# Probability transposes, value and relative matmuls of an attention loop placed one unit later in a hand-written order, and the output store one step later

## What is computed

```python
Q, K, V = (proj(Wq), proj(Wk), proj(Wv))             # 16 x 16 heads x 1024 x 16
scores = jnp.einsum('bhqd,bhkd->bhqk', Q, K) / SCALE
idx = clip(k - q, -256, 256) + 256
scores = scores + jnp.einsum('bhqd,qkd->bhqk', Q, pek[idx]) / SCALE
scores = jnp.where(causal[None, None], scores, -jnp.inf)
attn = jax.nn.softmax(scores, axis=-1)
out = jnp.einsum('bhqk,bhkd->bhqd', attn, V)
out = out + jnp.einsum('bhqk,qkd->bhqd', attn, pev[idx])
...
x = _layernorm(x + out @ Wo.T)
x = _layernorm(x + ffn(x))
```

## Time and profile before

| | |
|---|---|
| median of 3 runs | 5945.27 us (5935.37 to 5958.6) |
| the profiled execution | 5937.08 us; its span 5935.4 us |
| outside the span | 1.7 us |
| attention stage | from about 0.48 ms to 4.72 ms |
| busy over the span | PE 87%, DVE 64%, ACT 58%, POOL 31% |
| mean granted PE clock | 0.972 |

### The profile page before, as it was taken

How to read it: one execution, slowest core, us unless ns; L and a number is a source line. 1 busy time by engine, 2 the same in 40 slices (tenths; PEclk the granted TensorE clock), 3 DMA queues, 4 the chain that set the end, 5 groups by cost and what they waited for, 6 DMA issues and landing times. The chain is left out here.

```text
span 5935.4 us, 143051 instructions
## 1 busy us (share of the span) xinstructions
PE 5156.7 (87%) x49460; PEld 3407.6 (57%) x49460; DVE 3809.4 (64%) x8777; ACT 3447.7 (58%) x7512; POOL 1838.5 (31%) x2516
## 2 busy tenths in 40 slices
PE   9977888888888888888888888888888799999999
PEld 5545555555555555555555555555555556666655
DVE  5546676676667766676667666776677645555554
ACT  4436777777777777777777777777677511111111
POOL 4443333333333333333333333333333211111111
PEclk9989999999999999999999999999999999999999
DMA  7888999999999999899999999899999711111111
GB/s 225 253 225 278 287 299 292 285 294 297 287 290 294 302 292 298 286 292 295 294 290 294 290 293 291 289 296 296 283 293 291 248 54 57 57 57 57 57 57 39
DMA packets 653784, 1417.28 MB, mean 239 GB/s; under 512 B 64004, under 2 KB 362088, under 8 KB 640872
## 3 DMA queue, kind: packets, MB, share of 16 engines
q1 hardware_dynamic: 653160, 1409.10, 75.7%
HBM read 737.46 MB, written 671.35 MB: 237 GB/s over the span
## 5 line engine op out<-in xcount | busy, mean ns | idle before, releaser
L791 ACT ACTIVATE a_prob<-a_neg_s,a_neg_max 128x384 f32<-128x384 f32 (+1 forms) x1792 | 1076.1, 601 | 275.1 <-DVE a_neg_max L840 255.8
L511 DVE COPY a_p_t<-a_t_ps 128x512 f32<-128x512 f32 (+3 forms) x1536 | 954.3, 621 | 258.5 <-PE a_t_ps L755 251.9
L688 PE MATMUL a_s_ps<-a_k,a_q 96*128 96x512 bf16 (+3 forms) x3072 | 860.1, 334 | 192.8 <-ACT a_far L795 178.2
L762 PE MATMUL a_t_ps<-a_ident,a_band 128*128 128x128 f32 x3840 | 630.6, 285 | 384.3 <-DMA a_band<-prob_scr 359.4
L798 ACT ACTIVATE a_b_out<-a_t_ps 128x512 f32<-128x512 f32 (+1 forms) x1024 | 582.2, 569 | 635.9 <-PE a_t_ps L698 632.7
L840 DVE CUSTOM_DVE_ANT_1 a_neg_s<-a_s_ps,a_bias,a_far_neg 128x384 f32<-128x384 f32 x1280 | 791.1, 618 | 237.3 <-DVE a_far_neg L834 237.3
L755 PE MATMUL a_t_ps<-a_ident,a_prob 128*128 128x128 f32 x5120 | 865.4, 276 | 0.2 <-DVE a_p_t L511 0.2
L834 DVE TENSOR_REDUCE a_far_neg<-a_s_ps 128x1 f32<-128x640 f32 (+4 forms) x1280 | 708.9, 554 | 220.5 <-PE a_s_ps L688 120.9
L716 PE MATMUL a_o_ps<-a_p_t,a_v 128*32 128x128 f32 x18432 | 832.1, 294 | 0.2 <-ACT a_o_t L803 0.2
L798 ACT ACTIVATE a_p_t<-a_t_ps 128x512 f32<-128x512 f32 (+3 forms) x1536 | 669.7, 436 | 155.2 <-PE a_t_ps L755 151.4
L795 ACT ACTIVATE a_far<-a_s_ps,a_neg_max 128x640 f32<-128x640 f32 (+4 forms) x1280 | 732.4, 572 | 0.0
(11 more groups left out here) (99 smaller groups left out, 6660.9 us busy)
## 6 DMA issues: line engine op xcount, KB each, us to landing
a_bias<-bias_scr SPq DMA_DIRECT2D x448, 576.0 KB, 6.2
prob_scr<-a_prob SPq DMA_DIRECT2D x448, 576.0 KB, 7.1
bias_scr<-a_b_out SPq DMA_DIRECT2D x448, 512.0 KB, 4.0
a_band<-prob_scr SPq DMA_DIRECT2D x448, 512.0 KB, 6.1
qk_scr<-p_parts SPq DMA_DIRECT2D x256, 192.0 KB, 3.4
v_scr<-p_v_out SPq DMA_DIRECT2D x256, 128.0 KB, 2.2
a_v<-v_scr SPq DMA_DIRECT2D x64, 512.0 KB, 7.0
attn_scr<-a_o_t SPq DMA_DIRECT2D x512, 64.0 KB, 6.4
```

The costliest lines, as they stand in the source:

```text
L511: copy(p_t[par][:, u, blocks[0] * P:(blocks[-1] + 1) * P], bank[:, 0:len(blocks) * P]) \
L688: mm = pe.matmul(s_ps[:, u % 2, c:e], q_s[0:ROWS, g, u, qb * P:(qb + 1) * P], k_s[0:ROWS, g, u, c:e], start=True, stop=True)
L762: mm = pe.transpose(bank[:, n * P:(n + 1) * P], band_block(kk, 2 * i + n // 2, n % 2), ident[:, :])
L791: e = act.activation(near_prob(k, u, near(qb)), neg_s[:, u % 2, 0:w].rearrange("p (b c) -> p b c", c=P), ACT.Exp, bias=neg_max[:, u:u + 1] ...
```

## The change

All of the work behind the exponential is moved one unit later on the engines: the transposes of the probabilities of head h of tile k now stand five units behind the exponential (so that unit 0 of a step holds head 3 of the tile two back), the band transposes move from (unit 3, two steps back) and (unit 0, three back) to units 0 and 1, three back; the value parts and the relative matmuls with ACT's copy of the output move one unit too. The scores, the exponentials, the bias matmuls with their copies and all loads keep their places. The output store of a tile is issued at the end of the step after the one in which it stood, with a wait for `o_evac` that is met by then.

```diff
-    DEPTH = 4
+    DEPTH = 5
...
         BIAS_SLOTS = (0, 2)
-        BAND_SLOTS = ((3, 2), (0, 3))
-        VALUE_SLOTS = ((2, 2), (3, 2), (0, 3))
-        REL_SLOT = (1, 3)
+        P_LAG = 5
+        BAND_SLOTS = ((0, 3), (1, 3))
+        VALUE_SLOTS = ((3, 2), (0, 3), (1, 3))
+        REL_SLOT = (2, 3)
...
-                if ok(k - 1):
-                    jobs += [("p", u, k - 1, i) for i in range(len(t_banks(q_block(k - 1))))]
+                kp, head = k + (u - P_LAG) // GRP, (u - P_LAG) % GRP
+                if ok(kp):
+                    jobs += [("p", u, kp, i, head) for i in range(len(t_banks(q_block(kp))))]
...
-                    if k >= 0 and ok(k - 3):
-                        par = (k - 3) % 2
-                        qb, g = q_block(k - 3), ((k - 3) % TILES) // QB
-
-                        if not ok(k + LEAD):
-                            sp.wait_ge(o_evac, T - 2)
-                        row = attn[r_prev if k < 3 else r]
+                    if k >= 0 and ok(k - 4):
+                        par = k % 2
+                        qb, g = q_block(k - 4), ((k - 4) % TILES) // QB
+
+                        sp.wait_ge(o_evac, T - 3)
+                        row = attn[r_prev if k < 4 else r]
                         sp.dma_start(row[g, :, qb * P:(qb + 1) * P], o_t[:, par]).then_inc(stored[par], 16)
...
-                        if (u, 3) == REL_SLOT and ok(k - 3) and k >= 0:
+                        if u == REL_SLOT[0] and ok(k - 3) and k >= 0:
                             relative(r, k - 3)
...
-                        if u == 1 and ok(k - 3) and k >= 0:
+                        if u == REL_SLOT[0] and ok(k - 3) and k >= 0:
                             act.wait_ge(o_mm, T - 2)
```

More of the change, by code:

```diff
@@ L462, in plan @@
                 if ok(k + LEAD) and u in BIAS_SLOTS:
-                    jobs.append(("bias", u, k + LEAD, BIAS_SLOTS.index(u)))
-                if ok(k - 1):
-                    jobs += [("p", u, k - 1, i) for i in range(len(t_banks(q_block(k - 1))))]
+                    jobs.append(("bias", u, k + LEAD, BIAS_SLOTS.index(u), None))
+                kp, head = k + (u - P_LAG) // GRP, (u - P_LAG) % GRP
+                if ok(kp):
+                    jobs += [("p", u, kp, i, head) for i in range(len(t_banks(q_block(kp))))]
                 for i, (at, back) in enumerate(BAND_SLOTS):
                     if u == at and ok(k - back):
-                        jobs.append(("band", u, k - back, i))
+                        jobs.append(("band", u, k - back, i, None))
             return jobs
@@ L480, in wait_evac @@
         def wait_evac(eng, r, job):
-            kind, u, kk, i = job
+            kind, _, kk, i, head = job
             if kind == "band":
@@ L485, in wait_evac @@
             elif kind == "p":
-                who = t_engine(q_block(kk), u, i)
-                eng.wait_ge(t_evac[who], t_done(who, r, kk, u, i))
+                who = t_engine(q_block(kk), head, i)
+                eng.wait_ge(t_evac[who], t_done(who, r, kk, head, i))
             else:
@@ L499, in read_out @@
         def read_out(eng, copy, name, r, k, u, first, last):
-            for pos, (kind, uu, kk, i) in enumerate(plan(k, first, last)):
+            for pos, (kind, uu, kk, i, head) in enumerate(plan(k, first, last)):
                 if uu != u:
@@ L505, in read_out @@
                 by_head = bank.rearrange("p (h j) -> p h j", h=2)[:, :, j:]
-                if kind == "p" and t_engine(q_block(kk), u, i) == name:
+                if kind == "p" and t_engine(q_block(kk), head, i) == name:
                     blocks = t_banks(q_block(kk))[i]
-                    eng.wait_ge(t_mm, t_made(r, kk, u) - len(t_banks(q_block(kk))) + i + 1)
+                    eng.wait_ge(t_mm, t_made(r, kk, head) - len(t_banks(q_block(kk))) + i + 1)
                     if valid(kk - 2, first, last):
                         eng.wait_ge(pv_mm, TILES * r + kk - 1)
-                    copy(p_t[par][:, u, blocks[0] * P:(blocks[-1] + 1) * P], bank[:, 0:len(blocks) * P]) \
+                    copy(p_t[par][:, head, blocks[0] * P:(blocks[-1] + 1) * P], bank[:, 0:len(blocks) * P]) \
                         .then_inc(t_evac[name], 1)
@@ L742, in body @@
                         for pos, job in enumerate(jobs):
-                            kind, uu, kk, i = job
+                            kind, uu, kk, i, head = job
                             if uu != u:
@@ L752, in body @@
                             elif kind == "p":
-                                pe.wait_ge(exp_ready, 4 * (TILES * r + kk) + u + 1)
+                                pe.wait_ge(exp_ready, 4 * (TILES * r + kk) + head + 1)
                                 for n, b in enumerate(t_banks(q_block(kk))[i]):
                                     mm = pe.transpose(bank[:, n * P:(n + 1) * P],
-                                                      prob_block(kk, u, b), ident[:, :])
+                                                      prob_block(kk, head, b), ident[:, :])
                                 mm.then_inc(t_mm, 1)
```

## The result

The changed kernel took 5944.33 us (median of 20 runs, 5926.34 to 5956.64) and the kernel before, beside it, 5958.36 us (20 runs). The ratio is 0.9975, with an interval of 0.9964 to 0.9987. The profiled execution took 5935.27 us with a span of 5933.5 us, where the one before had 5935.4 us. The forecast was 5847 us. The time lies inside the range that was given, but the gain is a sixth of the one forecast, and smaller than the 0.5% that the prediction took as the least it could tell from no change.

A forecast was written before the change was run, and what follows sets the result against it. The prediction took transfers and engines to limit the attention in turn. Its terms, -0.7 (a), -1.0 (b and c) and +0.3 (d), gave -1.4 us a round, -90 us from 5937 to 5847 us, range 5760 to 5985 us.

The forecast's parts named there:

- What bounds the kernel: Attention: transfers limit steps 1 to 3, engines limit steps 0 and 6; 4.7 us a round of DMA dry time.
- (b): Steps 6, 7 and 0: more transfers queued on entry shrink dry time, at most 2.1 us a round; 1.0 taken after (c).
- the floor's distance: All DMA dry time of the attention, 64 x 4.7 = 300 us, the most any placement removes; floor at 5637 us.
- (a): Band transposes one unit, 2.08 us, later after their load: PE's wait mostly covered, 0.7 us a round gained, bounds 0 to 1.4.
- (c): Output store one step later: ACT's output copy waits in steps 1, 2 and 4, 2.2 us a round, 140 us in all.
- SP's new wait: SP's wait for the output copy, said to be met a step before and to cost nothing.
- (d): Head 3's transposes and a third of value work move to the next step: +0.3 us a round, bounds 0 to 0.8.
- The sum: -0.7 - 1.0 + 0.3 = -1.4 us a round, -90 us over 64 rounds, giving 5847 us.
- The first: Rival: stored-output wait moves earlier with the transfers, full unit gained, 3.5 us a round, 5713 us; chance 0.15.
- The second: Rival: transfers limit everywhere that matters, band wait becomes waits for store and bias load, 5937 to 5950 us; chance 0.20.
- The third: Rival: ACT's wait for the stored output in steps 1, 2 and 4 costs engine time, +1.3 us a round, 6020 us; chance 0.18.

The follow-up runs named there:

- e13_heads_back: e2_store_back with probability transposes back to four units behind the exponential, two value parts in unit 3, the last in unit 0: 5730.15 us, ratio 0.9646.
- e3_band_only: The kernel before with only the first half of the band transposes moved one unit later, beside the second half: 5771.53 us, ratio 0.9705.
- e4_store_late_only: The kernel before with only its output store issued one step later: 6371.41 us, ratio 1.0702.
- e5_lag_and_band: e3_band_only with the transposes of the probabilities also one unit later (`P_LAG = 5`): 5866.47 us, ratio 0.9845.
- e1_four_buffers: The changed kernel with four output buffers instead of two: 5870.46 us, ratio 0.986.
- e2_store_back: The changed kernel with the output store issued at the end of the step in which the output is copied, as before: 5870.79 us, ratio 0.9871.
- e10_banks_swapped: e2_store_back with the two banks of a heavy tile's probability transposes in the other order: 5861.93 us, ratio 0.9879.
- e6_bands_in_unit0: e2_store_back with both halves of the band transposes in unit 0: 6050.63 us, ratio 1.0157.

## Why the prediction missed

**What bounds the kernel** was right in the main: two limits in turn, with the DMA engines full in steps 1 to 5 and dry in 6 and 0, and 4.7 us of dry time a round to win. Step 7, which (b) names with 6 and 0, has a DMA share of 1.00 in the round of the earlier trace rows and is full. Kernel e13_heads_back took 218 us of the 300 us said to be the floor's distance.

**(a), the band's delay**, was right in mechanism: the wait fell from 359 to 0.3 us, and in the rounds shown the dry time of step 3 closed (share 0.96 to 1.00) and its clock came back (0.85 to 1.00). What it is worth with the store and the heads in their old places is 185 us, 2.9 us a round (e3_band_only); the prediction's (a) at 0.7 and (b) at its full 2.1 make 2.8.

**(b) and (c), the store**, were right in place and size, 138 us of ACT waits against 140, and the price came out as well: (b) had been cut from 2.1 to 1.0 us a round for it, 70 us, and taking the wait away gave 74. The 1.0 was picked out of a range of 0.5 to 2.1, so this agreement is partly luck. The text also argued that the waits in steps 1, 2 and 4 do not let the DMA engines run dry; half of their 138 us was time all the same. In e4_store_late_only, where they are five times as long, the DMA share fell to 0.85: ACT's wait holds PE's values, and the next transfers with them. The argument by a fixed cost of 2 us, set against (c), used a figure that its page states for GpSimd's DMAs. SP's new wait for the output copy was said to be met; it came to 11.1 us in all (788 to 4450 us).

**(d), the work moved between steps**, is the step that failed. It was taken at +0.3 us a round with a bound of 0.8. Putting only the transposes one unit later (e5_lag_and_band against e3_band_only) cost 95 us, 1.5 us a round, five times the value taken and nearly twice the bound. The same comes out without the store's wait: e1_four_buffers lies 86 us, 1.3 us a round, under its kernel before; with (a) at -0.7 and (b) at its full -2.1, this leaves +1.5 for (d). By e2_store_back against e13_heads_back, where the value parts move too, it is 141 / 64 = 2.2 us a round. It was priced by the duration of four transposes, as if only PE's sum of work counted. What changed as well is who waits for whom: in the changed order PE reaches a bank while DVE still has a maximum ahead of the copy, and the waits of the bias matmuls for DVE grew from 77.5 to 519.4 us. The sentence "the three banks keep as many jobs per pair of steps" is true (8 + 12 before, 9 + 11 after) and beside the point. The banks are not taken in one unbroken turn: `pos % RING` counts afresh in every step. With 11 jobs in a light step in place of 12, the first bias job of a heavy step takes a bank filled two jobs before, and no longer three.

The prediction named this case itself: "if the share stays at 0.93 with no band wait (then the engines are the limit, and (d) was mis-sized)". The share stayed at 0.93 and the band wait was gone.

**The sum** then reads -0.7 - 1.0 + 1.5 = -0.2 us a round, 13 us, where 14 us were measured between the medians. That agreement is partly built in, since (d) was taken from runs, and partly luck, since runs some 10 us apart can't tell 0.2 us a round from nothing. The chances of the verdicts don't quite follow from those of the cases: the cases add up to 0.22 for the same and 0.18 for slower, where 0.21 and 0.19 were given.

**The rivals.** The first did not come about in the changed kernel. Its gain was there to be had, though: it asked for 5713 us, and e13_heads_back, with the transposes in their old place and the store no longer late, took 5730. The second had the right time for the changed kernel, same within 0.5%, but for another reason: not because the band wait turns into a wait for transfers, but because gain and loss in different steps cancel. The third had the mechanism of the store, at 74 us, but the gain beside it was larger than the 1.2 us a round that it allowed.

**What stays open.** The edit `P_LAG = 5` costs 95 us, shown by e3_band_only against e5_lag_and_band, and 98 us with the transfers cut (one run each); the 141 us of e13_heads_back, and the 163 us of its pair with cut transfers, are of two edits. That it does so through DVE's copies is argued from timelines and waits and not shown; e10_banks_swapped only showed that it isn't one bank's wait. The edit also changes the number of jobs in a step, and with it the bank that each job gets. A kernel with the lag and a ring that runs on across steps would tell the two apart; it was not run, and neither was one with a fourth bank. Why e6_bands_in_unit0 is 180 us slower than e2_store_back wasn't followed up.

## What to carry to other kernels

When one piece of a hand-written order waits, move that piece alone first: here the band alone gave 3.0% and the whole rear part 0.25%. Then add the other pieces one by one: with both band halves, the relative values and the first value part a unit later, but the transposes and the store in their old places (e13_heads_back), the gain was 3.5%. Before moving work in an order with few buffers in turn, list for each job which copy frees its buffer, what stands ahead of that copy on its engine, and how much of PE's work lies between. Give each output buffer at least the queue's full landing time, and not the time of its own bytes.

## What was not expected of the hardware

A 64 KB store that is late is dear: 756 us of ACT waits made the kernel 7% slower. The store pays for what is ahead of it: 6.4 us to land, and 3.8 us when the four transfers through DRAM move a quarter of their bytes. And a PE stall has its price twice: in both rounds shown, the step with or right behind a long stall had a granted clock under 1 (0.85 in step 3 before, 0.82 in step 0 after), and it moved with the stall.
